# Who stores the parted weight blocks: from the sync queue to the engine that parts them

## The reference, cut to what matters

```
x = x + conv_mixer_0(channel_norm(x))      # pool to 9 tokens an image, a small state-space scan, upsample
t = tokens(x);  t = t + ffn_0(token_norm(t))   # 4 experts, token i goes to expert i % 4
x = x + conv_mixer_1(channel_norm(x))
t = tokens(x);  t = t + moe_1(token_norm(t))   # 8 experts, top 2 by a router
```

## Time and profile before

| | |
|---|---|
| median of three runs | 1184.3 us (1183.5 to 1186.58) |
| profiled execution, its own time | 1183.99 us |
| its span, first to last instruction | 1182.2 us |
| mean granted TensorE clock | 0.936 |
| busy, share of the span | PE 88%, weight loads 74%, DVE 60%, ACT 40%, POOL 36% |
| stores of parted blocks | 48, 1 MB each, from SP |

### The profile page before, as it was taken

The page is one execution under the profiler, slowest core; times in us unless marked ns, Lnnn a source line. Parts: engine busy times, 40 slices in busy tenths (PEclk is TensorE's granted clock), DMA queues, the critical chain, the costliest instruction groups (busy, mean ns, idle before and its releaser), DMA issues. The chain is left out here.

```text
span 1182.2 us, 18262 instructions
## 1 busy us (share of the span) xinstructions
PE 1040.3 (88%) x5916; PEld 874.7 (74%) x5916; DVE 713.6 (60%) x1411; ACT 476.2 (40%) x987; POOL 427.2 (36%) x446
## 2 busy tenths in 40 slices
PE   6877787889889997789979999799969999999986
PEld 3555687879888697689977677567857888888864
DVE  5776757986656468768675433765557334444327
ACT  3372236423234245226504335633642344443333
POOL 1105627863762115212212332622431443433421
PEclk9976789999999999999989999999978999999995
DMA  8426738776796366355744547542761689996578
GB/s 275 163 68 245 255 105 278 260 247 236 251 349 244 117 219 243 135 185 210 268 181 158 180 175 267 188 160 91 285 240 45 223 327 335 354 336 210 184 254 306
DMA packets 94664, 261.61 MB, mean 221 GB/s; under 512 B 10041, under 2 KB 48409, under 8 KB 78705
## 3 DMA queue, kind: packets, MB, share of 16 engines
q1 hardware_dynamic: 59800, 173.78, 41.2%
q0 software_dynamic: 14624, 48.64, 11.7%
q10 hardware_dynamic: 20152, 38.02, 10.2%
HBM read 168.59 MB, written 91.82 MB: 220 GB/s over the span
## 5 line engine op out<-in xcount | busy, mean ns | idle before, releaser
L655 POOL TENSOR_TENSOR sb_ring<-sb_raw,sb_ring 128x256 fp32r<-128x256 f32 x192 | 172.7, 931 | 191.0 <-ACT sb_ring L1223 163.2
L716 PE MATMUL ps<-sb_xnH,sb_ring 128*128 128x288 f32 x512 | 163.7, 320 | 18.8 <-DVE sb_sg L1799 7.2
L679 POOL DMA_INDIRECT y_dram<-sb_ysb,sb_target x86 | 86.2, 1003 | 246.2 <-ACT sb_ysb L1308 229.3
L1009 PE MATMUL ps<-sb_w,sb_xtH 128*128 x344 | 153.1, 445 | 13.4 <-DVE sb_hh L1851 11.5
L717 PE MATMUL ps<-sb_xnH,sb_ring 128*128 128x288 f32 x512 | 155.4, 304 | 0.0
L718 PE MATMUL ps<-sb_xnL,sb_ring 128*128 128x288 f32 x512 | 154.8, 302 | 0.0
L1844 DVE TENSOR_TENSOR sb_xtL<-ps,sb_xtH 128x512 fp32r<-128x512 f32 x86 | 59.3, 690 | 144.2 <-ACT sb_xtH L1288 144.1
L1011 PE MATMUL ps<-sb_w,sb_xtH 128*128 x344 | 138.1, 401 | 0.0
L1010 PE MATMUL ps<-sb_w,sb_xtL 128*128 x344 | 137.9, 401 | 0.0
L716 PEld LDWEIGHTS ps<-sb_xnH,sb_ring 128*128 128x128 f32 x512 | 100.5, 196 | 24.5 <-issue 8.5
L670 POOL DMA_INDIRECT sb_xs<-xn_dram,sb_source x86 | 88.1, 1024 | 51.7 <-DVE sb_source L1755 26.5
(11 more groups left out here) (246 smaller groups left out, 2304.1 us busy)
## 6 DMA issues: line engine op xcount, KB each, us to landing
w_dram<-sb_ring SPq DMA_DIRECT2D x48, 1024.0 KB, 5.1
sb_w<-w_dram SPq DMA_DIRECT2D x48, 1024.0 KB, 7.3
sb_ring<-w_dram SPq DMA_DIRECT2D x24, 1024.0 KB, 6.8
sb_raw<-in_w_ffn SPq DMA_DIRECT2D x24, 512.0 KB, 5.9
sb_raw<-in_w_ffn SPq DMA_DIRECT2D x48, 256.0 KB, 5.0
sb_X<-in_x SPq DMA_DIRECT2D x16, 576.0 KB, 8.8
sb_g<-y_dram ACTq DMA_DIRECT2D x18, 512.0 KB, 7.4
xn_dram<-sb_XN ACTq DMA_DIRECT2D x14, 512.0 KB, 5.1
```

The source lines that it names most:

```text
L655: last = pool.tensor_tensor(to[:, 1, cut], raw[:, i % RING, 1, cut], to[:, 0, cut].bitcast(f32), ALU.subtract)
L679: pool.indirect_dma_start(y_dram[h], bass.IndirectOffsetOnAxis(ap=target[:, h, m:m + 1], axis=0), ysb[:, r, :], None).then_inc(y_stored[r] ...
L716: pe.matmul(out_ap, w[0], xh, start=start, stop=False)
L1009: pe.matmul(PS[:, 1, :], xtH[:, i % 2, k, :], wh, start=k == 0, stop=False)
```

## The change

SP no longer stores parted blocks: `STORE`, `store_parted` and its calls in `weights` are gone, and SP's list holds loads only. POOL issues the store itself, right behind the fourth piece of the low part, after a wait for its own `lo_done`. The DMA moves the same bytes between the same places and counts the same semaphore.

```diff
-STORE = 6
...
-            def store_parted(r):
-                _, q, n, i = splits[r]
-                sp.wait_ge(lo_done, r + 1)
-                to = w1_dram[n] if q is None else w0_dram[q]
-                sp.dma_start(to, ring[:, i % RING, :, :].bitcast(f32)).then_inc(ring_stored[i % RING], 16)
-
             def weights():
-                parted = 0
                 for i, (slot, q, n) in enumerate(places):
-                    while parted < len(splits) and splits[parted][0] + STORE <= slot:
-                        yield splits[parted][0] + STORE
-                        store_parted(parted)
-                        parted += 1
                     yield slot
                     place_free(sp, i)
...
-                while parted < len(splits):
-                    yield splits[parted][0] + STORE
-                    store_parted(parted)
-                    parted += 1
...
                     last.then_inc(lo_done, 1)
+                    pool.wait_ge(lo_done, r + 1)
+                    pool.dma_start(w1_dram[n] if q is None else w0_dram[q], to.bitcast(f32))\
+                        .then_inc(ring_stored[i % RING], 16)
```

## The result

| | before | after |
|---|---|---|
| median, runs side by side | 1185.44 us (4 runs) | 1203.24 us (4 runs) |
| ratio, 95% interval | | 1.017, 1.0145 to 1.0195 |
| profiled execution, its own time | 1183.99 us | 1201.19 us |
| its span | 1182.2 us | 1199.4 us |

The time lies outside the predicted range of 1181 to 1195: the sign was right, the size was not. By the medians the loss is 17.8 us, by the ratio about 20, where 4.1 were forecast.

What follows compares the result with a forecast made beforehand. PE was taken as the bound in layer 0's first half; store delays of 0.76 + 0.44 + 1.93 + 0.93 = 4.06 us took the profiled 1183.99 to 1188.05, forecast as a median of 1188.4 us, range 1181 to 1195.

Steps and rivals of the forecast that it cites:

- (c): Blocks q4 to q10: an earlier p6 load gains 2.3 us, four stores delay the third `db` pair; net +0.44 us.
- (d): Blocks q22, p14, q23: stores delay low parts, PE stalls longer at q23, perhaps at a lower clock; +1.93 us.
- The price, 0.93 us: Each store on POOL: 0.15 us idle before, 0.75 issue, 0.03 after; 0.93 us.
- no change: Rival: the issue is as cheap as SP's, 0.56 us a store, total +0.1, 1184.4 us; chance 0.28.
- (a): Blocks p0 to p5: six stores fit in POOL's 5.7 us of idle time; 0 us.
- (b): Blocks q1 to q3: three stores outlast POOL's idle time, so `MR`, on PE's path, is late; +0.76 us.
- the 2.3 us at `Bb`: Blocks q4 to q10: p6's earlier load lets ACT issue `Bb`, and the first `db` start, 2.3 us earlier.
- (e): Block p16: its store delays `pRS`, and PE waits for pooling weights made of it; +0.93 us.
- faster: Rival: at q4 to q10 low parts escape DVE's scans and get shorter, 1180.7 us; chance 0.12.
- much slower: Rival: DVE holds up POOL's issue, 1.53 us a store, total +10.1, 1194.4 us; chance 0.15.

Runs made afterwards that it cites:

- experiment 12: Kernel before, plus on POOL behind every low part a wait and two one-column products, each with a wait, no DMA: 1192.36 us, ratio 1.0066.
- experiment 2: Kernel before, plus on POOL behind every low part a wait and an 8 KB DMA that nobody reads: 1197.98 us, ratio 1.0120.
- experiment 7: Changed kernel, but SP keeps its old waits for low parts without the stores, so loads go out no earlier: 1204.39 us, ratio 1.0170.
- experiment 9: Kernel before, with each low part as one product of 1024 columns instead of four of 256: 1195.66 us, ratio 1.0090.
- experiment 5: Changed kernel, plus a one-column product and a wait for it behind each store on POOL: 1198.71 us, ratio 1.0115.
- experiment 6: Kernel before, plus an 8 KB DMA on POOL behind each low part, then a one-column product and its wait: 1195.95 us, ratio 1.0091.
- experiment 3: Changed kernel, but ACT issues the 48 stores instead of POOL, six slots behind the block's slot: 1195.09 us, ratio 1.0093.
- experiment 13: Kernel before, with each low part as eight products of 128 columns instead of four of 256: 1189.16 us, ratio 1.0053.

## Why the prediction was wrong

**The step that failed** is the cost of a store. Each was priced as a delay of what is "queued behind the store on POOL", and DVE's instructions were taken to last as long as before. The sum has no term for POOL's products, once behind a DMA issue, no longer letting DVE in between them. That term is missing in (c): slots 16 to 48 grew by 10.6 us, of which the delay alone makes 2.9. A second step is mis-sized, (d): slots 80 to 96 grew by 6.5 us, and by 4.8 with the delay alone, where 1.93 had been forecast.

In loss by ratio, of some 20 us: experiment 12 puts the delay at 0.66% (7.8 us, by its interval 4 to 12, where the sum had 4.1), a little low, as its delay is a little short. Experiment 2, with the holds, lies 0.54% (6.4 us) above it. The change with SP's old order, experiment 7, lies another 0.5% (6 us) above experiment 2. Each of these differences is uncertain by some 0.4%. That holds cost time without any delay on POOL is shown by experiment 9, that taking them away gives time back by experiment 5. The last 6 us are not explained. Experiments 7 and 2 differ in the 1 MB stores on POOL's queue, but by the profiles the difference lies in slots 80 to 96 (38.8 against 32.8), and that stretch takes 36.3 in experiment 12 and 36.7 in experiment 6, where SP stores as before.

Then the terms, one by one.

*The price, 0.93 us.* Right as a sum, 0.89, but with luck: the issue took 0.57 us, not 0.75, and the wait in front 0.30, not 0.15. The rival "no change", which had 0.56 for all of it, falls; its guess at the issue itself was nearer, but it left out the wait.

*(a) 0, (b) +0.76.* Right in size. PE's wait behind q3, 1.49 us in the earlier trace rows, is now:

```profile
145.70 0.48 PE L836 MATMUL ps<-sb_rmb,sb_mats 128*128 128x288 f32 x1 [2.04 <-POOL sb_rmb L618]
```

+0.55. PE came to slot 0 1.6 us late, but 1.2 of that had come before the first store: POOL's first low part began at 96.67, against 95.46 before. By slot 16 all of it was made up (174.43 in the earlier trace rows, 174.40 now), at a clock of 1.00 in place of 0.91.

*(c) +0.44.* The load of p6 went out at 174.07, as forecast, and ACT's 3.93 us of the earlier trace rows are gone. But the 2.3 us at `Bb` were not won:

```profile
185.84 0.74 ACT L1114 ACTIVATE sb_dx<-ps,sb_vinn 128x72 f32<-128x72 f32 x3 [2.65 <-PE ps L779]
186.46 1.07 ACT L1210 ACTIVATE sb_ring<-sb_raw 128x1024 fp32r<-128x1024 f32 x1
186.92 0.34 ACTq L1118 DMA_DIRECT2D sb_Bb<-bc_dram  x1
```

ACT now waited for PE, which the hold at 175.60 had made late, and `Bb` was issued at 186.92 as against 186.71. Nor was the gain there without holds: in experiment 3, which loads p6 as early, at 176.90, the table was slow to land, and `Bb` went out at 189.98, 13.3 us behind the start of slot 16, against 12.3 before. Without that gain the working gave +2.74; the delay alone, in experiment 12, cost 2.9 there. So the delay was priced about right for this stretch, the gain was not there, and some 7.7 us, most of it holds, were missing. The third `db` pair, 0.44 us late by the forecast against 221.31 in the earlier trace rows, was 4.65 late:

```profile
225.96 3.88 POOL L604 TENSOR_TENSOR sb_db<-sb_dx,sb_Bb 128x576 f32<-128x576 f32 x2
```

*(d) +1.93.* Mis-sized. Slots 80 to 96 grew by 6.5 us, and by 4.8 with the delay alone. q23 was late, as forecast, but its low part then fell beside DVE's long multiplies. On POOL:

```profile
362.05 5.98 POOL L639 TENSOR_TENSOR sb_ring<-sb_raw,sb_ring 128x256 fp32r<-128x256 f32 x4 [1.19 <-ACT sb_ring L1210]
```

On DVE:

```profile
362.76 2.23 DVE L1766 TENSOR_TENSOR sb_xr<-sb_X,sb_rmb 128x1152 f32<-128x1152 f32 x1
...
365.97 1.47 DVE L1771 TENSOR_TENSOR sb_xr<-sb_xr,sb_rmb 128x1152 f32<-128x1152 f32 x1
```

That low part took 4.7 us before, 6.0 now, and 6.0 in experiment 12. Here POOL is the one that waits. PE's stall, 1.37 us in the earlier trace rows, is now 3.49, and the clock fell behind it:

```profile
368.08 0.61 PE L703 MATMUL ps<-sb_itH,sb_ring 128*128 128x288 f32 x1 [3.49 <-POOL sb_ring L639]
```

```profile
368.00:372.00 4.00, 3.92 (x16) 3.92 (x17) 0.00 (x0) 1.70 (x2) 0.99 (x3) 0.50 0.87 270
```

A granted 0.50 is the level of 1.2 GHz. I had given that half a chance and 0.8 us. In experiment 2 the same stretch grew by 1.2 us only, with the clock at 0.95, and in experiment 13, where POOL issues nothing new, it took 37.7: a term that small things turn over can't be priced to a microsecond.

*(e) +0.93.* The wait came as worked out, 2.11 in the earlier trace rows to 3.10:

```profile
417.63 0.65 PE L731 MATMUL ps<-sb_xtok,sb_RI 128*72 128x512 f32 x1 [3.10 <-DVE sb_RI L1392]
```

The stretch grew by 2.65, because PE's busy time grew too, from 51.03 to 52.69, at a clock of 0.97 in place of 1.00. The stall of 2.11 us had cost no clock there; behind the one of 3.10 it was 0.86 from 418 to 430 us. Over the three stretches of the first table PE's busy time went from 143.70 to 151.99 us for the same matmuls, 8.3 us, and the rows show no other cause than the clock. That is a large part of the loss (slots 0 to 16 gave 2.5 us of it back). It goes with the stalls, though no run changed the clock alone: experiment 12, in which PE stalls less, stands at 148.53.

*The rival "faster"* had the low parts win back what DVE took from them. They did get shorter, by 10 us, but DVE waited in their place; with the delay and no holds, in experiment 12, they took 176.3 us and won nothing.

*The rival "much slower"* came nearest in time, 1194.4, but by a mechanism that isn't there: no issue took over 0.74 us, where it had 1.35 (1.53 with what stands beside it). The contention I cited ran the other way. The traces show that a DVE instruction with two inputs in SBUF and a product of POOL don't run side by side, and that in the kernel before the loser waits for one instruction (0.90 us at 296.34). The Trainium skill, "SBUF — State Buffer", section "Who interferes with whom", has this rule: such a DVE instruction contends with a GpSimd instruction that reads SBUF, and the order of issue decides who waits until the other is done. On the kind of instruction the trace agrees. On the length it doesn't, behind a store: by the rule a wait is one product, some 0.7 us, and measured were 2.7 to 5.1 us, a run of four and, at 205.26, the rest of a run of six products. Nor do the starts fit it at 248.31, where DVE's instruction had begun before the run. The measurement decides.

What stays open: why a run behind an issue is not interrupted (shown is only that it takes an issue straight in front, of whatever size, and that a short product with a wait undoes it); why slots 80 to 96 take anything from 31.5 to 42.2 us in these runs, and with that the last 6 us (near them the loads of half blocks took 7.5 us by the median against 5.0 before, but no experiment changed that alone); and the split of the 20 us to better than some 5 us.

## What to carry to other kernels

When work is moved to an engine, price not only its delay but what its instructions do to a neighbour that shares SBUF access with it: look up in the trace who waits for whom now, and ask whether the move turns that order round. An issue on POOL straight in front of products that run beside DVE's two-input instructions is worth a look at DVE's longest instructions, not at their mean: here the median stayed at 0.46 us while five of 64 took 2.7 to 5.1. And a wait that looks large on a queue engine, like SP's 258 us, can be worth nothing: putting it back, in experiment 7, left the time as it was.

## What was new about the hardware

A DMA issue on POOL followed at once by products held DVE's two-input instructions to the end of the run (2.8 us for four products, 5.06 for the rest of six), unless DVE was at such an instruction when the run began (then 1.74 us, behind one product). It held even one that began 0.42 us before the run's first product. Without the issue DVE came in behind one product (0.90 us). The size of the DMA, 8 KB or 1 MB, made no difference to that: 5.01 and 5.06 us at the longest. POOL's issue took 0.56 us by the median for either.
